# Graph network kernel in two layers: edge blocks of 42 nodes, node products regrouped to full height, two edge tiles per PSUM bank

## The reference

```python
# layer 0: messages from node dst to node src; W1..W4 couple node and edge features (8 scalars, 8 vectors)
tp  = concat(xs es W1 + (xv . ev) W2, xs ev W3 + xv es W4)      # 160 per edge, scaled
agg = segment_sum(tp @ Wm + bm, src)
x   = layernorm(x + x + concat(x, agg) @ Wu + bu)
# layer 1: messages from node src to node dst
l0, l1 = x0 @ W_l1_0, x1 @ W_l1_1          # times node attribute a
w = relu(len10 @ W_fc1) @ W_fc2            # 192 weights per edge, in 64, 64, 32, 32
m0, m1 = w0 l0[src] e0, (w1 l0[src]) e1    # 64, 64 x 3
m2, m3 = (w2 e0) l1[src], w3 (l1[src] . e1)
s0..s3 = segment_sum(m, dst)
o0 = s0 @ W_l2_00 + s3 @ W_l2_10;  o1 = s1 @ W_l2_01 + s2 @ W_l2_11
x  = layernorm(x + si(x) + 0.5 a (o0, o1))
```

## Time and profile before

| what | value |
|---|---|
| median of 3 runs | 3978.24 us (3974.26 to 3978.79) |
| the profiled execution, its own time | 3976.29 us |
| its span, first to last instruction | 3974.6 us |
| busy: PE, PE weight loads, DVE | 3159.4 us (79%), 2467.6 us (62%), 2079.3 us (52%) |
| busy: ACT, POOL | 773.7 us (19%), 1813.8 us (46%) |
| mean granted TensorE clock | 0.923 |
| DMA | 641.02 MB, mean 161 GB/s |

### The profile page before, as it was taken

One profiled execution on the slowest core, in us unless ns is written; L12 is line 12 of the kernel. 1 busy time (PEld: TensorE's weight loads), 2 busy tenths in 40 slices (PEclk: granted clock), 3 DMA queues, 4 the chain that ended last, 5 costly groups with the idle time before them and its releaser, 6 DMA issues. The chain is left out here.

```text
span 3974.6 us, 61198 instructions
## 1 busy us (share of the span) xinstructions
PE 3159.4 (79%) x16014; PEld 2467.6 (62%) x16014; DVE 2079.3 (52%) x5812; ACT 773.7 (19%) x2531; POOL 1813.8 (46%) x2039
## 2 busy tenths in 40 slices
PE   0888838888888888887999867887878777777776
PEld 0333317777777777777888746665666556566664
DVE  3778864444444444444555545554555555555545
ACT  0333311111111111111111112221212122222111
POOL 1222215666666666662000065555555555555553
PEclk9999999999999999999999878888888888888888
DMA  7677758878887877874555332222222222222222
GB/s 287 283 316 307 313 192 230 228 227 231 228 230 227 231 227 229 231 224 174 196 203 200 117 72 64 67 63 66 63 64 66 63 65 66 65 67 67 63 63 77
DMA packets 493313, 641.02 MB, mean 161 GB/s; under 512 B 87161, under 2 KB 419541, under 8 KB 479782
## 3 DMA queue, kind: packets, MB, share of 16 engines
q1 hardware_dynamic: 130090, 308.44, 22.0%
q10 hardware_dynamic: 278124, 183.18, 16.8%
q0 software_dynamic: 84800, 145.68, 13.5%
HBM read 410.34 MB, written 226.72 MB: 160 GB/s over the span
## 5 line engine op out<-in xcount | busy, mean ns | idle before, releaser
L1311 POOL DMA_INDIRECT f_y<-y_table,b_rec x980 | 937.5, 957 | 1167.1 <-DMA b_rec<-in_records 461.4
L1087 PE MATMUL z_bank<-big,work 128*128 x6272 | 1008.9, 314 | 166.5 <-issue 101.2
L1087 PEld LDWEIGHTS z_bank<-big,work 128*128 128x128 f32 x6272 | 900.5, 196 | 274.3 <-issue 269.8
L855 POOL DMA_INDIRECT placed<-message,slots_now x784 | 762.8, 973 | 502.3 <-ACT message L1156 312.4
L963 DVE SCALAR_TENSOR_TENSOR work<-z_bank,quarter_node,work 128x512 f32<-128x512 f32 x784 | 534.2, 744 | 689.3 <-remote 333.0
L1468 PE MATMUL e_bank<-f_msg,f_hot 128*128 128x320 f32 x1960 | 786.4, 486 | 41.2 <-issue 26.7
L1372 DVE TENSOR_TENSOR f_msg<-e_bank,f_y 128x128 f32<-128x128 f32 x980 | 282.7, 289 | 626.1 <-PE e_bank L1461 329.8
L1461 PE MATMUL e_bank<-fc,b_hidden 100*128 100x192 f32 x1960 | 547.4, 364 | 0.0
L1461 PEld LDWEIGHTS e_bank<-fc,b_hidden 100*128 100x128 f32 x1960 | 399.5, 217 | 120.4 <-issue 36.6
L1468 PEld LDWEIGHTS e_bank<-f_msg,f_hot 128*128 128x128 f32 x1960 | 394.5, 215 | 53.3 <-issue 34.5
L1156 ACT COPY message<-z_bank 128x160 f32<-128x160 f32 x784 | 209.8, 296 | 946.0 <-PE z_bank L1087 720.1
(11 more groups left out here) (217 smaller groups left out, 2771.6 us busy)
## 6 DMA issues: line engine op xcount, KB each, us to landing
big<-products ACTq DMA_DIRECT2D x49, 3200.0 KB
products<-g SPq DMA_DIRECT2D x50, 2560.0 KB, 7.5
big<-placed SPq DMA_DIRECT2D x49, 1458.0 KB, 6.8
work<-in_e_t SPq DMA_DIRECT2D x784, 64.0 KB
b_lengths<-length_parts ACTq DMA_DIRECT2D x588, 37.5 KB
placed<-zeros SPq DMA_DIRECT2D x1, 15876.0 KB, 49.9
f_y<-y_table,b_rec POOLq DMA_INDIRECT x980
placed<-message,slots_now POOLq DMA_INDIRECT x784
```

Source lines behind the costliest of these rows:

```text
L855: pool.indirect_dma_start(v.placed[:, :], bass.IndirectOffsetOnAxis(slots_now[tile // SET % SLOT_SETS][:, tile % SET:tile % SET + 1], 0), ...
L1087: last = pe.matmul(p_msg[q][:, 0:D], spread[h % 2][:, j, q * P:q * P + P], windows[:, bass.ds(slot + j, 1), :].rearrange("p a b -> p (a b) ...
L1311: pool.indirect_dma_start(f_y[:, tile % Y_RING, :], None, v.y_table[:, :], bass.IndirectOffsetOnAxis(b_rec[b % REC_RING][:, j, 0:1], 0)).t ...
```

## The change

Three parts. **Layer 0, edges**: TensorE, ACT and the semaphores between them go by pairs of tiles. The messages of two tiles lie side by side in one bank, six banks are used, and there are three `spread` buffers. ACT copies 320 columns at once. **Layer 0, nodes**: x and the sums are multiplied in three products over 128, 128 and 97 rows; the result is turned in two pieces of 128 columns (the second overlaps the first) and multiplied in two products over 128 rows, with zeros in `w_nodes`. The new rows are also stored to `own_table`. **Layer 1**: 149 blocks of 42 nodes with 6 tiles each. A tile's sums are two products of 126 rows by 160 columns, one with attributes 0 to 2 (`level`), one with 1 to 3 (`turned`). Work goes in pairs of tiles, with other leads and deeper rings. Three blocks make a group of 126 nodes; its `combine` has six products of 128 rows and a bank of its own. `grouped` and `grouped_a` hold the nodes in groups of 126, loaded from `own_table` and an input `a_groups`; 50 groups are normalised at the end.

```diff
+PAIRS = TILES // 2
...
-TPB = 5
+TPB = 6
 BLOCK_EDGES = TPB * P
 HALF = BLOCK_EDGES // 2
-SUB = 32
-SUBS = P // SUB
+SUB = 42
+SUBS = 3
+GROUP = SUBS * SUB
+GROUPS = -(-NODES // GROUP)
 TAIL = CHUNK * P
-SMALL_BLOCKS = SUBS * FAST_BLOCKS
+SMALL_BLOCKS = -(-NODES // SUB)
...
+        v.w_nodes = sb("w_nodes", [P, 320])
...
-        v.w_post = sb("w_post", [P, 384])
+        v.w_post = sb("w_post", [P, 480])
...
+                load(v.w_nodes[0:S, 0:128], t["w_node0"])
+                load(v.w_nodes[64:96, 128:192], t["w_node1"])
+                load(v.w_nodes[96:128, 192:256], t["w_node1"])
+                load(v.w_nodes[96:128, 256:320], t["w_node1"])
...
-                load(v.w_post[S:P, 64:96], t["w_out1"][0:S, :])
...
-                load(v.w_post[0:32, 256:320], t["w_out0"][S:96, :])
-                load(v.w_post[32:64, 320:384], t["w_out0"][S:96, :])
-                sp.wait_ge(zeroed, 3)
+                load(v.w_post[64:96, 64:96], t["w_out1"][S:96, :])
+                load(v.w_post[96:128, 96:128], t["w_out1"][S:96, :])
...
+                load(v.w_post[96:128, 416:480], t["w_out0"][S:96, :])
+                sp.wait_ge(zeroed, 4)
...
+                chain.link(dve.tensor_scalar(starts[:], starts[:], float(EDGES), None, ALU.min))
...
+        SPREADS = 3
+        IDS_LEAD = 6
...
-        p_msg = bank[0:4]
+        p_pair = bank[0:4] + bank[6:8]
...
+                    sp.dma_start(v.own_table[at, :], v.own[:, bass.ds(i * N + k, 1), :].rearrange("p a d -> p (a d)")).then_inc(stores[k], 16)
...
-                    dve.wait_ge(expanded, batch * BATCH + 12)
+                    if batch >= SPREADS:
+                        dve.wait_ge(expanded, (batch - SPREADS + 1) * 2)
                     for j in range(WINDOW):
-                        last = dve.scalar_tensor_tensor(spread[h % 2][:, j, :], p_node[h % 2][:], v.quarter_node[:, j:j + 1],
+                        last = dve.scalar_tensor_tensor(spread[batch % SPREADS][:, j, :], p_node[h % 2][:], v.quarter_node[:, j:j + 1],
...
-                        pe.transpose(p_turn[k % 2][0:33, 1, :], agg[k][:, P:MW], v.ident[:]).then_inc(sums_full, 1)
+                        pe.transpose(p_turn[k % 2][:, 1, :], agg[k][:, P:], v.ident[:]).then_inc(sums_full, 1)
...
-                    pe.matmul(p_h[k % 2], xs[k][:], v.wu_s[:], start=True, stop=False)
-                    pe.matmul(p_h[k % 2], xv[k][:], v.wu_v[:], start=False, stop=False)
+                    pe.matmul(p_h[k % 2], x_main[k][:], v.wu_main[:], start=True, stop=False)
...
-                    pe.matmul(p_h[k % 2], at_b[k][:], v.wmu_b[:], start=False, stop=True).then_inc(h_full, 1)
+                    pe.matmul(p_h[k % 2], tail[k][:], v.w_tail[:], start=False, stop=True).then_inc(h_full, 1)
...
-                    pe.transpose(p_xn[k % 2][0:S, 0, :], xn_parts[k][:, 0:S], v.ident[:])
-                    for c in range(3):
-                        last = pe.transpose(p_xn[k % 2][0:V, 1 + c, :], xn_parts[k][:, S + 32 * c:S + 32 * c + 32], v.ident[:])
-                    last.then_inc(xn_full, 1)
+                    pe.transpose(p_xn[k % 2][:, 0, :], xn_parts[k][:, 0:P], v.ident[:])
+                    pe.transpose(p_xn[k % 2][:, 1, :], xn_parts[k][:, V:D], v.ident[:]).then_inc(xn_full, 1)
...
-                    pe.matmul(p_out[k % 2][:, 0:128], xn_s[k][:], v.w_node0[:], start=True, stop=True)
-                    for c in range(3):
-                        last = pe.matmul(p_out[k % 2][:, 128 + 64 * c:192 + 64 * c], xn_v[k][:, c, :], v.w_node1[:], start=True, stop=True)
-                    last.then_inc(outs_full, 1)
+                    pe.matmul(p_out[k % 2][:, 0:256], xn_t[k][:, 0, :], v.w_nodes[:, 0:256], start=True, stop=True)
+                    pe.matmul(p_out[k % 2][:, 256:320], xn_t[k][:, 1, :], v.w_nodes[:, 256:320], start=True, stop=True).then_inc(outs_full, 1)
...
+                    batch, bank_now = pair // 2, p_pair[pair % len(p_pair)]
+                    if pair % 2 == 1:
+                        load_word(batch + 1)
                     if k == 0:
                         pe.wait_ge(chunk_in[i % 2], 16 * (i // 2) + 16)
-                    pe.wait_ge(built, i * 4 + h + 5)
-                    pe.wait_ge(copied, tile + 1)
-                    for j in range(WINDOW):
-                        last = pe.matmul(p_msg[q][:, 0:D], spread[h % 2][:, j, q * P:q * P + P], windows[:, bass.ds(slot + j, 1), :].rearrange("p a b -> p (a b)"),
-                                         start=(j == 0), stop=(j == WINDOW - 1))
+                    pe.wait_ge(built, batch + 1)
+                    if pair >= len(p_pair):
+                        pe.wait_ge(copied, pair - len(p_pair) + 1)
+                    for n in range(2):
+                        q = pair % 2 * 2 + n
+                        slot = nc.s_assert_within((words[batch] >> (8 * q)) & 127, 0, 2 * SPAN - WINDOW)
+                        for j in range(WINDOW):
+                            last = pe.matmul(bank_now[:, n * D:n * D + D], spread[batch % SPREADS][:, j, q * P:q * P + P],
+                                             windows[:, bass.ds(slot + j, 1), :].rearrange("p a b -> p (a b)"), start=(j == 0), stop=(j == WINDOW - 1))
                     last.then_inc(expanded, 1)
 
-                unrolled(pe, TILES, CHUNK, (8, spread_ids), (4, expand))
-                pe.wait_ge(copied, U + TILES)
+                unrolled(pe, PAIRS, CHUNK // 2, (IDS_LEAD, spread_ids), (2, expand))
...
+                def copy_pair(i, k):
+                    pair = i * (CHUNK // 2) + k
+                    tile, at = 2 * pair, 2 * pair % TILE_RING
+                    if pair % 2 == 0:
                         for n in range(BATCH if tile >= TILE_RING else 0):
-                            act.wait_ge(scattered[(tile + n) % TILE_RING], 16 * (tile // TILE_RING))
-                        act.copy(message[:, k % TILE_RING:k % TILE_RING + 4, MW:RW], v.local[:, bass.ds(tile, 4)].unsqueeze(2))
-                    act.wait_ge(expanded, tile + CHUNK + 1)
-                    act.copy(message[:, k % TILE_RING, 0:D], p_msg[q][:, 0:D]).then_inc(copied, 1)
-                    if k == CHUNK - 1 and i + 2 < CHUNKS:
+                            act.wait_ge(scattered[at + n], 16 * (tile // TILE_RING))
+                        act.copy(message[:, at:at + BATCH, MW:RW], v.local[:, tile:tile + BATCH].unsqueeze(2))
+                    act.wait_ge(expanded, pair + 1)
+                    act.copy(message[:, at:at + 2, 0:D], p_pair[pair % len(p_pair)][:, 0:2 * D].rearrange("p (n d) -> p n d", n=2)).then_inc(copied, 1)
...
-        R = 10
+        R = 12
         Y_RING = 16
-        LENGTHS_RING = 4
+        LENGTHS_RING = 6
+        HIDDEN_RING = 3
         REC_RING = 8
+        COLUMNS = 4
...
-        p_bhid, p_trans, p_rad, p_acc, p_res = bank[0], bank[1], bank[2:6], bank[6:8], bank[1]
+        p_bhid, p_trans, p_res, p_rad, p_acc = bank[0], bank[1], bank[2], bank[3:6], bank[6:8]
...
+                for b in range(REC_RING):
+                    load_block(b // SUBS, b % SUBS)
+                last = NODES - (GROUPS - 1) * GROUP
...
+                sp.dma_start(v.grouped_a[:], t["a_groups"]).then_inc(own_in, 16)
...
+                    if pair >= Y_RING // 2:
+                        pool.wait_ge(weighed, pair - Y_RING // 2 + 1)
+                    for n in range(2):
+                        tile, j = 2 * pair + n, 2 * (pair % BPP) + n
+                        pool.indirect_dma_start(f_y[:, tile % Y_RING, :], None, v.y_table[:, :],
+                                                bass.IndirectOffsetOnAxis(b_rec[b % REC_RING][:, j, 0:1], 0)).then_inc(y_in[tile % Y_RING], 16)
...
+                    w = p_rad[pair % 3][:, 0:384].rearrange("p (t x) -> p t x", t=2)
+                    for n in range(2):
+                        dve.wait_ge(y_in[at + n], 16 * (2 * pair // Y_RING) + 16)
+                    dve.wait_ge(rad_full, pair + 1)
+                    dve.tensor_tensor(f_msg[:, r:r + 2, :, 0:S], w[:, :, 0:128].rearrange("p t (g c) -> p t g c", g=2),
+                                      f_y[:, at:at + 2, 0:S].unsqueeze(2).broadcast_to([P, 2, 2, S]), ALU.mult)
+                    for n in range(2):
+                        last = dve.tensor_tensor(f_msg[:, r + n, :, S:D].rearrange("p g (i c) -> p g i c", i=3),
+                                                 w[:, n, 128:192].rearrange("p (g c) -> p g c", g=2).unsqueeze(2).broadcast_to([P, 2, 3, V]),
+                                                 f_y[:, at + n, S:D].rearrange("p (i c) -> p i c", i=3).unsqueeze(1).broadcast_to([P, 2, 3, V]), ALU.mult)
+                    last.then_inc(weighed, 1)
...
+                    if pair >= 3:
+                        pe.wait_ge(weighed, pair - 2)
+                    for n in range(2):
+                        last = pe.matmul(p_rad[pair % 3][:, 192 * n:192 * n + 192], b_hidden[b % HIDDEN_RING][:, 2 * (pair % BPP) + n, :], v.fc2[:], start=True, stop=True)
```

(66 more changed lines are left out.)

326 lines of the change are left out of this document (165 added, 161 removed).

## The result

The changed kernel took 3675.7 us (median of 4 executions, 3672.5 to 3686.8) against 3978.5 for the kernel before: ratio 0.9245, 95% interval 0.9223 to 0.9266. It is faster, but by 303 us where I had forecast 668, and it lies outside my range of 3180 to 3600.

The account below looks back on a forecast made before the run. Halts and short-lead handshakes were taken to bound the edge stages, TensorE layer 0's nodes. Terms +2 - 160 - 88 - 420 + 1 = -665 took 3976 to 3311, given as 3310 us; range 3180 to 3600.

Parts of the forecast that it names:

- Setup and tail: Start and end of the kernel: more load issues on SP cost 2 us, one more closing subtraction under 1.
- Layer 0, nodes: Node stage: fewer, fuller products save 1.82 us a block, taken as -88 us; VectorE's chain stays hidden.
- Layer 0, edges: Edge stage: pairs and a longer TensorE lead absorb halts, -160 us, ends -218 and 0.
- A halt of 3.4 us: Layer 0's edges: ACT's unexplained 3.36 us wait for a product, to be covered by a lead of 12 tiles.
- TensorE's 1.14 us a tile: Layer 0's edges: TensorE's work for each tile, 890 us in all, so not the stage's bound.
- Rival (b): Layer 0's edges stay bound by TensorE or the windows' load: -60 instead of -160, kernel 3410 us; chance 0.08.
- Layer 1: Edge stage of layer 1: fewer tiles and longer leads bring 1670 us to 1250, -420, ends -520 and -140.
- rival (a): Layer 1's handshakes go on binding, halts and half clock persist: -140 to -250 there, kernel 3536 us; chance 0.26.
- A 3.4 us halt is then about covered: Layer 1: leads grown from one tile step (0.87 us) to nearly two pair steps (3.5 us) absorb a halt.
- the floor of the gathers plus 128 us for the rest: Layer 1: 894 gathers at 1.255 us make 1122 us; 28 for ramp and drain, 100 for halts and half clock.
- Rival (c): Layer 1: TensorE waits for gathers in every pair and stays at half clock, kernel slower at 4311 us; chance 0.03.

Follow-up runs that it names:

- e2: Changed kernel with POOL's indexed scatters and gathers replaced by SP transfers of fixed rows; layer 1 996 us for 1453, layer 0's edges 1405 us.
- e5: Changed kernel with POOL's index-driven DMAs replaced by direct DMAs of fixed rows, still issued by POOL; kernel 3015 us.
- e6: Changed kernel with 280 useless index-driven gathers of 128 rows added on POOL beside layer 0's nodes; that stage grew by 353 us.
- e1: Changed kernel with only layer 0's edge stage put back as before; that stage 1231 us, kernel 3718.1 us.
- e19: Changed kernel run again unchanged, in the other, faster kind of set; 3152.6 us against 3332.1 for the kernel before.
- e20: Kernel before, run again unchanged for its trace, in a set of the first kind; layer 0's edges 1214 us, nodes 424, layer 1 1647.
- e16: e5 with all layer 0 chunk loads but the first two left out; layer 0's edges 954 us.
- e3: Changed kernel with constant window slots in layer 0's edges and one combine product instead of six in layer 1; stages 1199 and 1445 us.
- e4: Changed kernel with layer 0's chunk loads after the first two and layer 1's length loads after 18 left out; 1246 and 1427 us.
- e17: Changed kernel with layer 0's edge products over two of the four window slots; that stage 1193 us.
- e11: e6 with rows of 8 bytes, and one pair in four of layer 1 loaded by SP; nodes 704 us, layer 1 1184 us.
- e14: Changed kernel with 144 paced gathers beside layer 0's nodes and one useless gather per pair in layer 1; 349 and 2065 us.
- e15: Kernel before with POOL's index-driven DMAs replaced by direct ones on POOL; layer 0's edges 1036 us, nodes 421, layer 1 1076.
- e21: e6 run again in another set; layer 0's node stage 689 us.
- e8: Changed kernel with layer 0's scatters replaced by SP stores of four tiles and every other layer 1 pair loaded by SP; layer 1 969 us.

## Why the prediction was wrong

- **Setup and tail**: forecast +3, measured +1 (first product of the edges) and under 1.
- **Layer 0, nodes**: right, -83 for -88, block 7.02 for 6.99. VectorE's chain stayed hidden, and the 97-row pair costs nothing.
- **Layer 0, edges**: wrong. The step that failed is "A halt of 3.4 us is then shorter than 12 tiles x 1.14 = 13.7 us, so POOL, with a backlog, becomes the bound at 1000 us". It took the halt as an event of fixed length from outside the loop. e2, e5 and e6 show that in sets of the first kind it comes with POOL's own index-driven DMAs, so a POOL that is never starved would keep everybody else waiting. With the old lead of 4 tiles (e1, 1231 us) and with 12 (1223) the stage takes the same. In the other kind of set the stage does run at POOL's 1000 us (e19), but by the estimate under e20 the kernel before does too, so that the -160 would be missing there as well. TensorE's 1.14 us a tile left out 0.08 for the node numbers (e16, 954 us for my 890), which was not what failed. Rival (b) gave -60 for a bound by TensorE or transfers; its size came nearer, its reason is excluded by e3, e4 and e17.
- **Layer 1**: -217 for -420, between the ends I gave (-520 and -140) and within rival (a)'s -140 to -250. Failed: "A 3.4 us halt is then about covered", and the floor of the gathers plus 128 us for the rest. POOL's free pitch of 1.255 us is a floor only where TensorE can report beside it (e19: 1146 us, even below my 1250); with late reports the 894 gathers cost 1453. What the gain of 217 is made of was not measured. Two parts are at hand: 86 fewer gathers (86 x 1.32 = 113 us, an estimate with the slope of e11 and e14), and less of TensorE's work (117 in e15 against e5). They add up to 230, but whether they add is not shown, and no run takes layer 1's blocks of 42 nodes apart from its longer leads.
- **Rival (a)** said that the handshakes go on binding; e2 and e5 show that the handshakes with the same leads cost nothing when reports are prompt. Its number was near, its mechanism only half right.
- **Rival (c)** did not come about: clock 0.88 in layer 1, and 0.99 in e19, where POOL's gathers do bound the stage. The clock goes with the halts: 0.53 in e6's stretch of 81 passes, 0.94 right behind it. The prediction had named for (c) what the Trainium skill, page TensorE: Matmul & The Clock Gate, section HAM oscillation, says of matmul bursts separated by DMA waits. In e19 TensorE's waits for VectorE, which needs the gathered rows, are 2.1 us at most and the clock stays up, so that case did not arise here.
- **The range** missed because I gave the forecast 0.57 with a halt that I could not name. Seen from now, it should have had a case in which the unnamed cause scales with POOL's DMAs and both edge stages keep their excess: 3976 - 88 - 140 to 250 = 3640 to 3750, which holds the 3676.

## What to carry to other kernels

If an engine's finished work is seen late by all others and the cause has no name, price it with a dose, not with a lead: take the suspected neighbour away in one run and add it where it was absent in another. Where POOL's index-driven DMAs run at full pace beside TensorE, count them first: here 86 fewer of them were worth some 110 us by an estimate, about what all the rest of layer 1's change is worth undisturbed (117), while layer 0's banks and leads were worth nothing (e1). An idle engine that waits for another's result is not free to be sped up if its own activity is what delays that result.

## What the runs showed of the hardware that was not expected

- Index-driven DMAs on POOL, one per 1.25 us, brought TensorE down to 81 passes in 200 us (e6; e21, in another set, has the same stage time within 7 us); direct DMAs of the same bytes from POOL did nothing of the kind (e5). Three at a time with a pause, one per 2.4 us on average, cost 349 us for 343 (e14), and 448 in layer 1 nothing (e8).
- TensorE's own instructions were held meanwhile: weight loads and passes 1.40 us apart, for 0.14 us from pass to pass otherwise (e6).
- The number of rows (32 or 128) and their length (8 or 648 bytes) made no difference to that (701, 704 and 696 us).
- In one set the same programs ran without these halts: 3152.6 us for 3675.7, and 3332.1 for 3978.5. The same kernel took 17 to 19% longer by something that no line of it names, so a change has to be compared within one set.
